# Cross attention on one core: the first pair of batches rewritten, and the second pair's low x input made by VectorE

## The reference

```python
text_p  = x   @ W_text  + b_text
audio_p = ctx @ W_audio + b_audio
Q = layer_norm(text_p, g1, beta1)
K = layer_norm(audio_p, g2, beta2)
alpha = softmax(Q @ K.T / sqrt(512))
H = (alpha @ audio_p) @ W_out + b_out
out = layer_norm(H + x, g_out, beta_out)
```

## Time and profile before

| what | us |
|---|---|
| median of 3 runs | 1273.65 |
| lowest and highest | 1273.39, 1273.81 |
| the profiled execution, its own time | 1272.33 |
| its span, first to last instruction | 1270.5 |
| TensorE busy | 1251.0 (98%) |
| VectorE busy | 1078.2 (85%) |
| ScalarE busy | 1053.8 (83%) |
| GpSimd busy | 547.4 (43%) |
| ScalarE and VectorE wait for the first data until | 7.56 and 5.55 |

### The profile page before, as it was taken

One profiled execution on the slowest core, in us unless ns is written; L12 is line 12 of the kernel. 1 busy time (PEld: TensorE's weight loads), 2 busy tenths in 40 slices (PEclk: granted clock), 3 DMA queues, 4 the chain that ended last, 5 costly groups with the idle time before them and its releaser, 6 DMA issues.

```text
span 1270.5 us, 22559 instructions
## 1 busy us (share of the span) xinstructions
PE 1251.0 (98%) x6648; PEld 1067.6 (84%) x6648; DVE 1078.2 (85%) x1726; ACT 1053.8 (83%) x1789; POOL 547.4 (43%) x545
## 2 busy tenths in 40 slices
PE   6999999999999999999999999999999999999997
PEld 5688888888888888888888888888888888888886
DVE  6678888988888988888888888888889888889888
ACT  6787888888888988888888888888888888888884
POOL 0113554335544335544345544345544355543356
PEclk9999999999999999999999999999999999999999
DMA  7257766768767678776678667688677687677793
GB/s 257 60 163 226 224 189 187 188 204 239 225 172 200 185 217 239 211 180 196 184 228 239 202 170 198 194 235 235 180 190 186 204 244 222 179 192 188 210 236 104
DMA packets 99013, 253.53 MB, mean 200 GB/s; under 512 B 12336, under 2 KB 28208, under 8 KB 90800
## 3 DMA queue, kind: packets, MB, share of 16 engines
q1 hardware_dynamic: 77632, 187.22, 42.1%
q0 software_dynamic: 21360, 66.06, 28.9%
HBM read 137.38 MB, written 49.81 MB: 147 GB/s over the span
## 4 chain that ended last, share of the span: by engine, by line
PE 95%; DVE 2%; DMA 1%; ACT 1%; SPq 1%; issue 0%; DVEq 0%; ACTq 0%; POOLq 0%
PE wide L328 9%; PE wide L327 9%; PE wide L324 9%; PE score L292 7%; PE score L294 7%; PE score L293 7%; PE wide L382 7%; PE wide L381 7%; PE wide L380 7%; PE wide L294 7%; PE wide L292 7%; PE wide L293 7%; PE turn L293 1%; PE turn L294 1%; PE turn L292 1%; PE turn L334 1%
## 5 line engine op out<-in xcount | busy, mean ns | idle before, releaser
L1121 POOL TENSOR_TENSOR y_rows<-y_rows,betao_row 128x512 f32<-128x512 f32 x120 | 167.0, 1391 | 332.5 <-ACT y_rows L583 219.4
L324 PE MATMUL wide<-xT_hi,wt_hi 128*128 128x512 f32 x512 | 202.1, 395 | 2.5 <-ACT k_cols L543 1.3
L328 PE MATMUL wide<-xT_hi,wt_lo 128*128 128x512 f32 x512 | 202.2, 395 | 0.0
L327 PE MATMUL wide<-xT_lo,wt_hi 128*128 128x512 f32 x512 | 201.9, 394 | 0.0
L292 PE MATMUL wide<-cT_hi,wa_hi 128*128 128x512 f32 x384 | 152.4, 397 | 0.0
L542 ACT ACTIVATE squares<-wide,bac_col 128x512 f32<-128x512 f32 x128 | 88.2, 689 | 77.3 <-PE wide L294 77.3
L294 PE MATMUL wide<-cT_hi,wa_lo 128*128 128x512 f32 x384 | 152.1, 396 | 0.0
L293 PE MATMUL wide<-cT_lo,wa_hi 128*128 128x512 f32 x384 | 151.9, 396 | 0.0
L382 PE MATMUL wide<-wao_hi,pcT_lo 128*128 128x512 f32 x372 | 146.7, 394 | 0.0
L380 PE MATMUL wide<-wao_hi,pcT_hi 128*128 128x512 f32 x372 | 146.6, 394 | 0.0
L381 PE MATMUL wide<-wao_lo,pcT_hi 128*128 128x512 f32 x372 | 146.5, 394 | 0.0
(11 more groups left out here) (145 smaller groups left out, 3505.0 us busy)
## 6 DMA issues: line engine op xcount, KB each, us to landing
xT_in<-in_xT SPq DMA_DIRECT2D x32, 1024.0 KB, 8.9
xT_lo<-xT_in POOLq DMA_DIRECT2D x31, 1024.0 KB, 8.9
y_rows<-in_x_rows SPq DMA_DIRECT2D x124, 256.0 KB, 4.1
y_rows<-bao_row POOLq DMA_DIRECT2D x31, 1024.0 KB, 9.5
out<-y_rows SPq DMA_DIRECT2D x124, 256.0 KB, 3.3
cT_in<-in_cT SPq DMA_DIRECT2D x32, 768.0 KB, 8.7
c_kept<-in_c_rows SPq DMA_DIRECT2D x32, 768.0 KB, 7.4
p_out<-probs SPq DMA_DIRECT2D x31, 512.0 KB, 4.6
```

The source lines that it names most:

```text
L324: nc.tensor.matmul(wide[h][:], wt_hi[:, d, cols], xT_hi[:, d, :], start=(d == 0), stop=False)
L327: nc.tensor.matmul(wide[h][:], wt_hi[:, d, cols], xT_lo[:, d, :], start=False, stop=False)
L328: done = nc.tensor.matmul(wide[h][:], wt_lo[:, d, cols], xT_hi[:, d, :], start=False, stop=(d == DT - 1))
L1121: nc.gpsimd.tensor_tensor(rows, rows, betao_row[:], ALU.add).then_inc(y_ready, 1)
```

## The change

1. **Loads in chunks.** W_audio and the first cT, and W_text and the first xT, come in DMAs of one chunk each (128 x 512, 256 KB), alternating, each with its own semaphore. The six bias and gain vectors are laid side by side by the host, and one DMA brings them (`cols`).
2. **K by chunks.** `first_k(d)` does chunk d for all four banks, then the next chunk. W_audio is transposed chunk by chunk (`turn_wa`) into score0, score1 and turn1. The means are made by chunk: for W_audio's chunks 1 and 2 by ScalarE (`wa_mean_of`, an activation that sums its row), else by VectorE.
3. **Q by parts.** `first_products` goes over chunks 0 to 2 of banks 0 and 1, then bank 2, then chunk 3 of all three, then the sum of K's squares, then bank 3. Half of the bias fold stands after the first Q piece and half after `fold_weights(0)`; it goes to score1. `fold_weights(1)` and `(2)` stand behind the sum of Q's squares.
4. **ScalarE and VectorE** have a written order of their own for the first pair (`first_casts`, `first_parts`); there each cast of x or W_text is followed by work on K.
5. **The second pair's xT_lo** is made by VectorE (`x_low(1, d)`: chunks 0 and 1 in the first step, 2 and 3 in the second); `xT_minus(1)` and `add_xT(1)` are gone, and every count that followed them is lower by one DMA. From pair 2 on nothing changes.
6. **Addresses.** `cols` takes 96 bytes a partition where six tiles of 32 were, four of them further down, and an unused tile `b_shift` of the size of those four fills the place. In the built programs all tiles but the small vectors (columns, means, bias sums) have the same address as before.

```diff
-            sp.dma_start(wa_stage[:, 0:CT, :], w_audio.rearrange("(t p) h -> p t h", p=P)).then_inc(wa_loaded, 16)
-            load_cT(0)
-            for to, of in columns:
-                sp.dma_start(to[:], of.rearrange("(t p) -> p t", p=P),
-                             allow_slow_non_contiguous=True).then_inc(columns_loaded, 16)
-            sp.dma_start(wt_stage[:], w_text.rearrange("(t p) h -> p t h", p=P)).then_inc(wt_loaded, 16)
-            load_xT(0)
+            for d in range(CT):
+                sp.dma_start(wa_stage[:, d, :], wa_of[:, d, :]).then_inc(wa_loaded[d], 16)
+                sp.dma_start(cT_in[:, d, :], cT[0, :, d, :]).then_inc(cT0_loaded[d], 16)
+                if d == 0:
+                    sp.dma_start(cols[:], columns).then_inc(columns_loaded, 16)
+            for d in range(DT):
+                sp.dma_start(wt_stage[:, d, :], wt_of[:, d, :]).then_inc(wt_loaded[d], 16)
+                sp.dma_start(xT_in[:, d, :], xT[0, :, d, :]).then_inc(x0_loaded[d], 16)
...
+            def first_k(d):
+                pe.wait_ge(cT_split, d + 1)
+                pe.wait_ge(wa_split, d + 1)
+                for h in range(HT):
...
+            turn_wa(0)
+            turn_wa(1)
+            first_k(0)
+            turn_wa(2)
+            pe.wait_ge(columns_loaded, 16)
+            nc.tensor.matmul(turn[0][:, 0:HT], ones, ba_col[:], start=True, stop=True)
+            nc.tensor.matmul(turn[0][:, HT:2 * HT], ones, bt_col[:], start=True, stop=True).then_inc(b_spread, 1)
+            first_k(1)
+            first_k(2)
...
+            def first_products():
+                first_q(0, 0)
+                fold_bias(range(HT // 2))
+                first_q(1, 0)
+                for d in range(1, DT - 1):
+                    first_q(0, d)
+                    first_q(1, d)
+                for d in range(DT - 1):
+                    first_q(2, d)
+                for h in range(HT - 1):
+                    first_q(h, DT - 1)
+                mean_squares(0, turn[0][:], k_sq_parts, k_var)
+                for d in range(DT):
+                    first_q(3, d)
+                fold_weights(0)
+                fold_bias(range(HT // 2, HT))
+                mean_squares(0, turn[1][:], q_sq_parts, q_var)
+                fold_weights(1)
+                fold_weights(2)
...
+            def wa_mean_of(d):
+                act.wait_ge(wa_loaded[d], 16)
+                nc.scalar.activation(squares[:, d, :], wa_stage[:, d, :], ACT.Identity, scale=-1.0 / H,
+                                     accum_out=wa_mean[:, d:d + 1]).then_inc(wa_averaged, 1)
...
+            def first_casts():
+                for d in range(1, DT):
+                    x0_high(d)
+                    k_centre(0, d - 1)
+                    wt_high(d)
+                k_centre(0, HT - 1)
+                cT_high(1, 0)
+                cT_high(1, 1)
+                move_half(0, turn[0], k_summed, k_moved)
...
+            for d in range(DT):
+                weights_mean(wt_stage, d, wt_mean, wt_loaded, wt_summed, wt_mean_made)
+                x_low(0, d)
+                weights_low(wt_lo, wt_hi, wt_stage, d, wt_mean, wt_hi_made, wt_split)
...
+                for h in range(HT):
+                    k_norm(0, h)
+                add_square(0, q_paired, q_squared, q_added)
+                sum_squares(0, q_squared, q_added, q_summed)
+                k_low(0, 0)
+                halve_sum(0, turn[1], q_moved, q_halved)
+                split_sum(0, k_var, 1, q_halved, q_sq_hi, q_sq_parts)
...
                 pair_squares(i, k_squared, k_paired)
+                if not late:
+                    x_low(i, 2)
                 add_square(i, k_paired, k_squared, k_added)
+                if not late:
+                    x_low(i, 3)
...
-                if not last:
+                if not first and not last:
                     add_xT(i + 1)
```

More of the change, by code:

```diff
@@ L1023, in step @@
                 maxima(i, 1)
-                if not first and not last:
+                if not last:
                     y_sum(j, 1 - odd, 3)
```

373 lines of the change are left out of this document (212 added, 161 removed).

## The result

The changed kernel takes 1266.62 us (median of 6 runs, 1265.89 to 1266.83), the kernel before beside it 1272.93 (6 runs, 1271.95 to 1273.81). The ratio is 0.995, with a 95% interval of 0.994 to 0.996: faster by 6.3 us. The profiled executions say 1266.83 against 1272.33, with spans of 1265.0 and 1270.5. Forecast were 1266.8 in the median and a gain of 6.9 between profiled executions; there it is 5.5. The changed kernel's profiled execution is the slowest of its six runs.

What follows compares the result with a forecast made beforehand. TensorE's matmuls were taken to bound the kernel, so gain lies only in its head and second-pair waits: 5.7 us earlier start plus 1.2 in the second pair, 6.9 in sum, median 1273.65 to 1266.75 (1266.8), range 1264.9 to 1269.8.

Steps and rivals of the forecast that it cites:

- First chunk: Head, loads: the first 256 KB chunk alone lands at 3.45 + 0.8 = 4.25 us.
- K: First pair: K starts at 6.9 against 10.51, with 1.6 for slow matmuls, and ends at 17.7 against 20.5.
- the rival of the later clock: Head: gaps between chunks keep TensorE slow until 13.7, 1.8 us worse; gain 5.1, 1268.6 us; chance 0.18.
- Q and its sums: First pair: Q ends at 31.2, no wait at K's sum, TensorE waits 0.6 at Q's sum, done at 37.1.
- Folds and scores: First pair's end: two folds 6.6, scores 6.16; second pair starts at 49.8, 5.7 us earlier.
- Second pair: Second pair: VectorE makes xT_lo in idle places, so TensorE's wait of 1.22 for the DMA goes; 1.2 us gained.
- The new wait on pT_lo: Second pair, rival: TensorE waits for the probabilities' low part; 0.5 of the 1.2 given back, 1267.3 us; chance 0.12.
- Loop: From the third pair on: same order on every engine and same addresses of large tiles, priced at 0.
- The same 39.2 us for a pair: Loop, sign in the changed profile: a pair still takes 39.2 us.
- A changed length of the loop's pairs: Loop: sign that the prediction is wrong, if the pairs change their length.
- Chunks: Loads to 22 us: 388 GB/s, 0.68 us a chunk, second pair's cT at 21.9; well under 388 means wrong.
- The third rival: ScalarE's cast of the second pair's cT: slow chunks delay K's sum; 1271.0 at 287 GB/s, 1275.5 at 240; chance 0.12.

Runs made afterwards that it cites:

- the five with the same first pair: The changed kernel, the one with the second pair's xT_lo by DMA again, and the three with moved tiles; second pair starts at 50.27 to 50.84 us.
- the experiment: Changed kernel with the second pair's xT_lo again made by ScalarE's negation and an adding DMA; median 1267.23 us, second pair 1.15 longer.
- early transposes: Changed kernel plus twelve transposes of the identity on TensorE while it waits for W_audio; median 1266.95 us, span 1265.2.
- the last kernel: Changed kernel with early transposes, VectorE's new orders, ScalarE's half of K's sum before the next cT's casts, bias fold two chunks later; median 1265.34 us.

## Why the prediction was right, step by step

- **First chunk**: 4.25 forecast, 3.39 measured. Both parts of the sum were too large: 262 KB had passed at about 2.9 (by the row in slices of 0.4) and not at 3.45, and they landed 0.5 later and not 0.8. The Trainium skill, "DMA: Bandwidth & Descriptors", section "Anatomy of one DMA — SWDGE (gpsimd) path", gave 3.3 by its figure for GpSimd's path; for this load, which SyncE issues, the trace agrees.
- **K**: start 6.9 forecast, 6.41 measured; end 17.7 against 17.96. The early start was taken back by the slow stretch: I charged 1.6 us for slow matmuls, it was 4.83 - 11 x 0.233 = 2.3. For the third transposes and the tiny matmuls I charged 0.7, where the halves of my own rows give 0.9; it was 0.80. The rival of the later clock (a rise at 13.7) didn't come, it rose at 11.24. Neither the 1.6 nor the rival's 1.8 belonged in the sum in full: K's end counts only as long as it, and not the second pair's cT, is what K's sum comes from. The Trainium skill, "TensorE: Matmul & The Clock Gate", section "Part 1: The HAM clock gate", says the count of slow matmuls varies from run to run of one kernel. The traces agree as far as they go: no kernel was profiled twice, but the five with the same first pair had 11, 9, 5, 9 and 7 slow distances in K.
- **Q and its sums**: Q's end 31.2 against 31.13; no wait at K's sum, as forecast; 0.97 at Q's in place of 0.6.
- **Folds and scores**: the start, 49.8 forecast, is 50.46: a gain of 5.06 and not 5.7. All of it is in the way to Q's sum: that was to be done at 37.1 and is at 37.75. The two folds took 6.47 and not 6.6, the scores 50.46 - 44.22 = 6.24 and not 6.16. K's sum was on time (28.07 against 28.1), but the four scalings of K end at 33.4 and not at 32.8, as ScalarE takes a bank of Q out before it turns to the sum:

```profile
28.66 0.70 ACT L596 ACTIVATE q_cols<-wide,btc_col 128x512 f32<-128x512 f32 x1
29.38 0.66 ACT L616 ACTIVATE turn<-turn,eps 128x512 f32<-128x512 f32 x1
...
30.69 2.72 DVE L916 SCALAR_TENSOR_TENSOR k_cols<-k_cols,cols,turn 128x512 f32<-128x512 f32 x4 [1.42 <-ACT turn L618]
```

- **Second pair**: 1.2 forecast, 0.92 measured, 1.15 by the experiment. The 0.26 left is VectorE's fourth piece, which stands behind an add that waits for ScalarE's square; I had called those places free. The new wait on pT_lo didn't come: it is done at 68.75 + 1.22 = 69.97 and asked for at 70.74.
- **Loop**: priced at 0; 0.56 was given back. "The same 39.2 us for a pair" was a misreading: 39.2 is the length of the stretches of the earlier trace rows, and a pair took 38.407. The experiments on addresses show that "all large tiles keep their addresses" carried 4 to 6 us, which the prediction used without having a price for it. A difference as small as 0.02 a pair also appears between kernels with one loop and one placement (38.404 to 38.436), so its cause stays open. A changed length of the loop's pairs was named as a sign of being wrong; a change no larger than that doesn't count as one.
- **Chunks**: the stretch ran at 209 to 313 GB/s to 10.5 us and at about 337 on the whole (26 chunks' worth in 20.2 us), not at 388. That was named as a sign of being wrong, and it was one: cT of the second pair landed at 23.59, where the prediction had 21.9, although the first chunk came 0.9 earlier than reckoned. It cost nothing in this execution because ScalarE asked at 23.64. That is luck. In the four other kernels with this first pair it landed 0.6 to 1.35 later, and ScalarE waited 0.33 to 2.17 for it. The third rival had the place right: as soon as TensorE and ScalarE are quicker, this load is the next wait (3.27 with early transposes, 1.93 in the last kernel). Its size was far smaller than that rival's, since the loads ran at about 400 GB/s behind 10.5 us.

By parts, from the experiments one at a time: loads in chunks 3.7, one column load for six 2.0 in the chunked head (each to within the 0.6 us of equal heads), K by chunks 0.3 to 0.9, xT_lo by VectorE 1.15, Q's order nothing that shows, the kept place of the tiles 4 (and 6 for the other slow one). They overlap and don't add up to 6.3.

The mechanism was right: the chain through K's sum and Q's sum moved as a whole, and the DMA for xT_lo was the second pair's wait. That the median came within 0.2 us was luck. The gain between profiled executions was over-forecast by 1.4 (0.64 at the start, 0.3 in the pair, 0.5 in the loop). It was made up for by 1.5: the profiled execution was taken to lie 1.3 under the median, and the changed kernel's lies 0.2 above it.

## What to carry to other kernels

Where a loop leaves its engine no gap, look for gain at the head, and load first the smallest piece with which the chain can start: it beat the load by whole tensors, which moved more bytes a second, by 3.7 us, and each tiny load ahead of it costs an issue. Before a slow clock or a reordering is priced, ask who waits next: 2.25 us won on TensorE here came to nothing because ScalarE waited for a load that stood at the end of the queue. Look at several executions before a difference of half a us in a head is believed. And keep the tiles where they lie when others are added, or compare kernels at several places, since a few bytes can hide or fake a gain of half a per cent.

## What the runs showed of the hardware

- Moving all large tiles but the weights by 32 to 96 bytes changed TensorE's pace by up to 0.5%, with no gap on it: 38.43 us a pair as they lay, 38.57 at 96 bytes lower, 38.63 at 32 higher, 38.42 at 64 higher. The last is the sum of a slower K and Q (8.404 and 11.201 against 8.364 and 11.158) and a quicker output part (8.262 against 8.356).
- 256 KB loads, the first ones issued 0.47 us apart, moved 209 to 313 GB/s over their first 9 us, whole loads of 786 KB and 1 MB in their place 333 to 440 from 3 to 19.5 us.
- The same head differs from one execution to another: with the same issues in the same order, the second pair's cT landed at 23.59 to 24.94, W_audio's second chunk at 5.47 to 6.20, and K had 5 to 11 slow distances.
- A bias-fold matmul followed by one of Q cost 0.4 us beyond the usual distance (19.97 to 20.61, against 0.233).
